# Graph attention over a random adjacency matrix: 2 MB adjacency loads, and a step whose parts stand in another order

## The chip, the cores and the metric

The kernel runs on one core of a Trainium2 chip. The number that counts is the device time of one execution in microseconds; where several runs were made, their median. The core's engines are TensorE (PE in the profile, its weight loads PEld), VectorE (DVE), ScalarE (ACT), GpSimd (POOL) and SyncE (SP), which only issues transfers here. Sixteen DMA engines move the data of all queues.

## The reference, cut to what matters

```python
h = relu(layernorm(x))                         # x: 8192 x 256, f32
support = (h @ weight)                         # 4 heads of 64 columns
f1 = support . weight_u; f2 = support . weight_v     # one number per node and head
scores = leaky_relu(f1[m] + f2[n], 0.2)        # for each pair n, m
masked = scores * adj                          # adj: 8192 x 8192, int32, ones with probability 0.000488
attn = softmax over m where masked != 0
out = attn @ support + bias + h @ proj_w.T + proj_b
return x + out
```

A row of the adjacency matrix has about four ones. The matrix itself has 8192 x 8192 x 4 bytes = 268 MB, and each byte of it is read once.

## The kernel before

The 8192 rows are worked in 64 tiles of 128 rows. All sizes of loads below are for 128 partitions.

**Reading the matrix.** SyncE issues `load_adj(t)` for each tile in order: four loads (`UNITS = 4`) of 1 MB, each with 8 KB for a partition, into six slots (`HELD = 6`). A slot can be loaded again when TensorE has read it. TensorE's `pack_places(t)` and `pack_unit(t, u)` turn the 8192 entries of a row into 1024 words by matmuls (16 for a tile, 4 for a unit), and the last matmul of a unit frees the slot (`s_adj_used`). VectorE's `pick_words(t)` finds the words that are not empty, and `split_words` makes columns of them.

**First stage** (up to about 230 us): sixteen times, four tiles of x are normalised, transposed and projected, the rows of `support` are stored in a table in HBM, and one tile of the matrix is packed beside it.

**Second stage**: 32 groups of two tiles (`GS = 2`), one group in each step `g` of the loop over `range(LATE)`, `LATE = 30`, and then two groups more, written out. In a step the engines work on four groups at a time:

- VectorE picks the one or two tiles that `picks[g]` names (2, 1, 2, 1, ..., and 2 in each of the last three), computes `one_hot(g)` and `list_spill(g)` for group g, `scores`, `row_maximum`, `shift` and `weigh` for g - 1, `output` for g - 2, and `list_own(g + 1)`, the indices of the first five neighbours of each row of group g + 1.
- TensorE computes `offsets(g)` and `edge_records(g)`, `row_scores(g - 1)`, `edge_refs(g - 1)`, `aggregate(g - 2, b)` (the weighted sum over a tile's gathered rows), and packs the tiles `t + 1` for `t` in `picks[g]`.
- GpSimd gathers rows of the table by indirect DMA: ten for a group by `gather_own` (five for each of the two tiles), after `list_own` and after ScalarE's `clear`, and two by `gather_spill`, after `list_spill`. Three groups of gathered rows (`RING = 3`) are held.
- ScalarE copies the edge records out of PSUM (`record_edges`), clears a ring slot, computes `distances(g + 1)` and the exponentials.

Each engine runs its part in the order in which it is written; semaphores tie the engines together. SyncE's stores of the output stand behind all loads of the matrix in its queue.

## Time and profile before

| | |
|---|---|
| median of 3 runs | 858.75 us (856.42 to 859.03) |
| the profiled execution | 857.76 us, of it a span of 855.9 us |
| TensorE busy | 712.2 us (83%) |
| VectorE busy | 644.8 us (75%) |
| GpSimd busy | 530.2 us (62%) |
| ScalarE busy | 129.5 us (15%) |
| moved by DMA | 329.82 MB, 385 GB/s over the span |
| of it SyncE's queue q1 | 286.28 MB, its packets 83.6% of the 16 engines' span |
| of it the gathers, q0 | 34.30 MB, 11.1% |

The profile gives an engine's busy time, the idle time in front of a group of instructions with what ended it, and for the DMA queues the packets, their bytes and the time that they took. A packet of the matrix is one partition's contiguous row of a load. The time of a packet runs until its data have moved, so a share of 1.00 says that each of the sixteen engines had a packet under way, and not at which rate.

### The profile page before, as it was taken

Reading aid. Unit: us, or ns where it says so; the run is one execution under the profiler, and the core shown is the slowest. Engines: PE = TensorE matmul, PEld = TensorE weight load, DVE = VectorE, ACT = ScalarE, POOL = GpSimd, SP = SyncE. Lnnn points to the kernel's source line nnn. Section 1 sums busy time; section 2 is a strip of 40 time slices with the busy share of each in tenths; the row PEclk is TensorE's granted clock in tenths of the full one; section 3 lists DMA queues with packets and bytes.
Section 4 is the critical chain, followed back from the end, with each engine's and each line's share of the span. In section 5 each row is a group of like instructions: output and inputs, shape, how many; then the busy total and the mean of one; then the engine's idle time right before and its main releaser. Section 6 shows DMA issues by size and latency. Waiting matters only on the chain.

```text
span 855.9 us, 11167 instructions
## 1 busy us (share of the span) xinstructions
PE 712.2 (83%) x3011; PEld 438.6 (51%) x3011; DVE 644.8 (75%) x2747; ACT 129.5 (15%) x468; POOL 530.2 (62%) x598
## 2 busy tenths in 40 slices
PE   2989999999957889777888888788888878888777
PEld 0656666666514454454545444455545445454455
DVE  4556666657446989879778797978879797889886
ACT  0223333333210001000001011000011100000010
POOL 4444455454467776776767667676776766676760
PEclk9999999999966879998888898887989899799888
DMA  8999999999999999999999999999999999999971
GB/s 317 419 417 396 415 409 420 416 420 406 425 408 393 385 397 394 401 405 393 399 387 376 389 370 398 384 406 388 397 396 381 403 382 407 378 384 388 404 308 51
DMA packets 63855, 329.82 MB, mean 385 GB/s; under 512 B 12795, under 2 KB 15560, under 8 KB 31024
## 3 DMA queue, kind: packets, MB, share of 16 engines
q1 hardware_dynamic: 43056, 286.28, 83.6%
q0 software_dynamic: 18432, 34.30, 11.1%
q10 hardware_dynamic: 2304, 8.52, 2.4%
q8 instruction: 25, 0.41, 0.2%
q14 instruction: 38, 0.31, 0.1%
HBM read 328.99 MB, written 16.91 MB: 404 GB/s over the span
## 4 chain that ended last, share of the span: by engine, by line
PE 44%; DVE 26%; DMA 23%; issue 3%; POOL 2%; ACT 1%; POOLq 0%; ACTq 0%; SPq 0%
DMA adj_raw<-in_adj 20%; PE ps_words L400 12%; PE ps_agg L461 9%; PE ps_agg L381 7%; PE ps_two L381 6%; DVE att L937 6%; PE ps_two L400 5%; DVE cand L791 3%; DVE base L947 3%; DMA att<-support_table,idx 2%; PE ps_score L445 2%; DMA att<-in_x 1%; PE ps_words L392 1%; DMA support_table<-att 1%; PE ps_list L371 1%
## 5 line engine op out<-in xcount | busy, mean ns | idle before, releaser
L719 POOL DMA_INDIRECT att<-support_table,idx x384 | 418.4, 1090 | 184.5 <-issue 105.0
L400 PE MATMUL ps_words<-adj_raw,pack_w 128*128 128x512 fp8e4 x640 | 187.0, 430 | 25.9 <-DMA adj_raw<-in_adj 25.9
L461 PE MATMUL ps_agg<-att,ident 128*128 128x260 f32 x640 | 183.0, 441 | 6.7 <-DVE att L937 6.7
L461 PEld LDWEIGHTS ps_agg<-att,ident 128*128 128x128 f32 x640 | 139.7, 225 | 41.6 <-issue 17.3
L400 PE MATMUL ps_two<-adj_raw,pack_w 128*128 128x512 fp8e4 x384 | 112.6, 442 | 22.2 <-DMA adj_raw<-in_adj 22.2
L400 PEld LDWEIGHTS ps_words<-adj_raw,pack_w 128*128 128x128 bf16 x640 | 62.3, 106 | 124.7 <-DMA adj_raw<-in_adj 38.9
L791 DVE MAX8 cand<-ps_words 128x8 f32<-128x128 f32 x320 | 67.2, 281 | 66.3 <-PE ps_words L400 66.3
L937 DVE TENSOR_TENSOR att<-att 128x1536 f32<-128x1536 f32 x64 | 109.6, 1751 | 1.2 <-ACT att L623 1.2
L710 POOL COPY record<-att 128x8 f32<-128x8 f32 x64 | 13.5, 212 | 116.9 <-ACT att L567 116.9
L400 PEld LDWEIGHTS ps_two<-adj_raw,pack_w 128*128 128x128 bf16 x384 | 38.5, 111 | 83.9 <-DMA adj_raw<-in_adj 31.8
L381 PE MATMUL ps_agg<-w_all,hT 128*128 128x260 f32 x256 | 63.0, 389 | 4.0 <-ACT hT L563 3.8
L381 PE MATMUL ps_two<-w_all,hT 128*128 128x260 f32 x256 | 62.0, 385 | 2.6 <-ACT hT L563 2.6
L947 DVE SCALAR_TENSOR_TENSOR base<-ps_agg,rdenom,base 128x64 f32<-128x64 f32 x256 | 55.0, 277 | 2.3
L381 PEld LDWEIGHTS ps_two<-w_all,hT 128*128 128x128 f32 x256 | 47.3, 190 | 11.3 <-ACT hT L563 3.1
L381 PEld LDWEIGHTS ps_agg<-w_all,hT 128*128 128x128 f32 x256 | 46.0, 190 | 13.4 <-ACT hT L563 7.8
L708 POOL TENSOR_TENSOR base<-att,bias_row 128x256 f32<-128x256 f32 x64 | 46.9, 733 | 0.1
L712 POOL TENSOR_TENSOR base<-base,att 128x256 f32<-128x256 f32 x64 | 46.6, 728 | 0.0
L791 DVE MAX8 cand<-ps_two 128x8 f32<-128x128 f32 x192 | 40.2, 280 | 6.2 <-PE ps_two L400 6.0
L617 ACT ACTIVATE edge_rec<-ps_list 128x34 f32<-128x34 f32 x32 | 6.4, 199 | 249.0 <-PE ps_list L438 249.0
L871 DVE TENSOR_SCALAR edge_slot<-edge_rec,edge_at 128x2 f32<-128x2 f32 x32 | 7.5, 234 | 47.2 <-ACT edge_rec L617 47.2
L445 PE MATMUL ps_score<-score_slot,onehotT 128*128 128x44 f32 x128 | 23.6, 322 | 19.6 <-DVE score_slot L903 19.6
L461 PE MATMUL ps_agg<-att,onehotT 128*128 128x260 f32 x128 | 39.0, 386 | 0.0
(118 smaller groups left out, 796.8 us busy)
## 6 DMA issues: line engine op xcount, KB each, us to landing
adj_raw<-in_adj SPq DMA_DIRECT2D x256, 1024.0 KB, 13.5
support_table<-att ACTq DMA_DIRECT2D x16, 520.0 KB, 8.7
att<-in_x SPq DMA_DIRECT2D x16, 512.0 KB, 6.4
out<-base SPq DMA_DIRECT2D x15, 512.0 KB, 15.1
att<-support_table,idx POOLq DMA_INDIRECT x384, 6.3
out<-base SPq DMA_DIRECT2D x4, 128.0 KB, 1.9
w_all<-in_proj_wT SPq DMA_DIRECT2D x2, 128.0 KB, 5.6
w_all<-in_weight SPq DMA_DIRECT2D x2, 128.0 KB, 5.8
```

Of the source, the lines that this page charges most:

```text
L371: mm = nc.tensor.transpose(ps_t[t % 2][:, c * P:(c + 1) * P], xhat[:, t // LOAD % 2, t % LOAD, c * P:(c + 1) * P], ident[:])
L381: mm = nc.tensor.matmul(ps_proj[t % 2][:, half, 0:ROW], hT[:, t % 2, c * P:(c + 1) * P], w_all[:, c, half, :], start=(c == 0), stop=(c == ...
L400: mm = nc.tensor.matmul(ps_words[buffer_of(t)][:, k * 512:(k + 1) * 512], pack_w[:, u * UT + s, :], adj_low[:, n % HELD, s, k * 512:(k + 1 ...
L445: mm = nc.tensor.matmul(ps_row[:, b].rearrange("p k h -> p (k h)"), onehotT[:, g % RING, b], score_slot[:, b].rearrange("p k h -> p (k h)" ...
L461: mm = nc.tensor.matmul(ps_agg[:, b, 0:ROW], ident[:] if k < OWN else onehotT[:, g % RING, b], gathered[:, g % RING, b, k], start=(k == 0) ...
L708: pool.tensor_tensor(base[:, t], x_in[:, g % 2, q, :], bias_row[:], ALU.add).then_inc(s_basev, 1)
L710: pool.tensor_copy(record[:, t, R_F2:].rearrange("p (a h) -> p a h", a=2), stage[:, g % 2, :, q, HF:])
L712: pool.tensor_tensor(base[:, t], base[:, t], stage[:, g % 2, 0, q, 0:HF], ALU.add).then_inc(s_based, 1)
L719: pool.indirect_dma_start(gathered[:, g % RING, b, k, :], None, table, bass.IndirectOffsetOnAxis(idx[:, g % RING, b, k:k + 1], 0), bounds_ ...
L791: last = v.max(cand[:, s * 8:(s + 1) * 8], ps[:, s * SEG:(s + 1) * SEG])
L937: v.tensor_tensor(r, r, rows[:, :, HF:].unsqueeze(3).to_broadcast([P, BLOCKS, H, HD]), ALU.mult).then_inc(s_weighted, 1)
L947: last = v.scalar_tensor_tensor(base[:, t, cols], ps_agg[:, b, cols], rdenom[:, b, h:h + 1], base[:, t, cols], ALU.mult, ALU.add)
```

## The change

- `UNITS = 2`, `HELD = 4`: a tile is loaded in two loads of 2 MB, each with 16 KB for a partition, and four slots hold 8 MB (before, six held 6 MB). A unit has 8 matmuls now. To make room, `spare`, `uv_row`, `projb_row` and `place_hi` lie in the last tiles of `base` and `hT` in `onehot`, which are not used at the same time.
- The order of a step for groups before `SOLO` (27): TensorE does `edge_records(g)`, both aggregations, `row_scores`, `edge_refs`, `offsets(g + 1)`, and packs last, now the tiles `t + 2`; tile 17 is packed before the loop. VectorE does `one_hot(g)` first, then picks, `list_spill(g)`, `scores(g - 1)`, and `list_own(g + 1)` in the middle of the step. ScalarE clears and does `distances(g + 1)` ahead of the exponentials.
- From group 27 on the two tiles of a group are listed, cleared and gathered singly; before, only the last two groups were.

```diff
-UNITS = 4
-HELD = 6
+UNITS = 2
+HELD = 4
...
+    AHEAD = [g for g in range(G) if FIRST + sum(counts[:max(g - 1, 0)]) >= groups[g][0] + GS]
+    SOLO = len(AHEAD)
+    assert AHEAD == list(range(SOLO)) and RING <= SOLO < LATE
+
+    def listed(g, b):
+
+        return g + 1 if g < SOLO else SOLO + GS * (g - SOLO) + b + 1
...
-        spare = sb("spare", [P, 4, HF])
...
-        uv_tmp = spare[:].rearrange("p (q c) d -> p q c d", q=2)
+
+        uv_tmp = base[:, TILES - 4:].rearrange("p (q c) d -> p q c d", q=2)
+        uv_row = base[:, TILES - 6:TILES - 4]
+        projb_row = base[:, TILES - 7]
+        place_hi = base[0:2, TILES - 9:TILES - 7].rearrange("p a d -> p (a d)").bitcast(BF16)
...
+        hT = onehot[:].rearrange("p a b m -> p a (b m)")
...
-                    if q > 0:
-                        pack_unit(g + 1, q - 1)
+                    if q > 0 and q % (LOAD // UNITS) == 0:
+                        pack_unit(g + 1, q // (LOAD // UNITS) - 1)
...
             pe.wait_ge(s_staged, TILES)
+            pack_places(FIRST + 1)
+            for u in range(UNITS):
+                pack_unit(FIRST + 1, u)
+            offsets(0)
             for g in range(LATE):
-                new = [t + 1 for t in picks[g]]
-                offsets(g)
-                pack_places(new[0])
-                for u in range(UNITS // 2):
-                    pack_unit(new[0], u)
-                if g >= 2:
-                    aggregate(g - 2, 0)
-                edge_records(g)
+                if g >= SOLO:
+                    offsets(g)
+                else:
+                    edge_records(g)
+                for b in range(GS):
+                    if g >= 2:
+                        aggregate(g - 2, b)
+                if g >= SOLO:
+                    edge_records(g)
                 if g > 0:
                     row_scores(g - 1)
-                for u in range(UNITS // 2, UNITS):
-                    pack_unit(new[0], u)
-                if g > 0:
                     edge_refs(g - 1)
-                if g >= 2:
-                    aggregate(g - 2, 1)
-                for t in new[1:]:
-                    pack_places(t)
-                    for u in range(UNITS):
-                        pack_unit(t, u)
+                if g + 1 < SOLO:
+                    offsets(g + 1)
+                for t in picks[g]:
+                    if t + 2 < TILES - 1:
+                        pack_places(t + 2)
+                        for u in range(UNITS):
+                            pack_unit(t + 2, u)
...
-                if g + 1 == LATE:
-                    clear(LATE, 0, 1)
+                if g + 1 >= SOLO:
+                    for b in range(GS):
+                        clear(g + 1, b, 1)
+                elif g + 1 >= RING:
+                    clear(g + 1)
+                if g + 1 < SOLO:
+                    distances(g + 1)
                 if g > 0:
                     exponential(g - 1)
-                if g + 1 == LATE:
-                    clear(LATE, 1, 1)
-                elif g + 1 >= RING:
-                    clear(g + 1)
-                distances(g + 1)
+                if g + 1 >= SOLO:
+                    distances(g + 1)
...
-            def gather_own(g, n, at=0, size=GS):
-                pool.wait_ge(s_idx_own, n)
-                pool.wait_ge(s_cleared, n)
-                for b in range(at, at + size):
+            def gather_own(g, *only):
+                for b in only or range(groups[g][1]):
+                    pool.wait_ge(s_idx_own, listed(g, b))
+                    pool.wait_ge(s_cleared, listed(g, b))
                     for k in range(OWN):
                         gather(g, b, k)
...
-            for g in range(LATE - 1):
-                gather_own(g, g + 1)
-                gather_spill(g)
...
+            for g in range(SOLO):
+                gather_own(g)
+                if g + 1 < SOLO:
+                    gather_spill(g)
+            for g in range(SOLO, G):
+                gather_own(g, 0)
+                gather_spill(g - 1)
+                gather_own(g, 1)
+            gather_spill(G - 1)
...
             list_own(0)
             for g in range(LATE):
+
+                due = [t for t in picks[g] if g + 1 >= SOLO and t < groups[g + 2][0]]
+                if 0 < g < SOLO:
+                    one_hot(g)
+                if g + 1 >= SOLO and groups[g + 1][0] < picks[g][0]:
+                    list_own(g + 1, 0, 1)
                 n = pick_words(picks[g][0], 0)
-                if g + 1 == LATE:
-                    picked = split_words(picks[g][0], 1, n)
-                    list_own(LATE, 0, 1)
+                if due:
+                    picked = split_words(due[0], 1, n)
+                    list_own(g + 1, due[0] % GS, 1)
                 if g == 0:
 
                     dve.wait_ge(s_based, TILES)
-                one_hot(g)
+                if g == 0 or g >= SOLO:
+                    one_hot(g)
+                else:
+                    list_spill(g)
                 if g > 0:
                     scores(g - 1)
-                list_spill(g)
+                if g == 0 or g >= SOLO:
+                    list_spill(g)
+                if g + 1 < SOLO:
+                    list_own(g + 1)
+                if g >= 2:
+                    output(g - 2, 0)
                 if g > 0:
                     row_maximum(g - 1)
-                if g >= 2:
-                    output(g - 2, 0)
...
-                    list_own(g + 1)
```

What the order of instructions shows, for a step in the middle of the second stage. TensorE before, one step with two new tiles (`ps_list<-spilled` is `offsets`, `ps_words<-adj_raw` a pack, `ps_agg` an aggregation, `ps_list<-record` is `edge_records`, `ps_score` first `row_scores` and then `edge_refs`):

```order
L429 MATMUL ps_list<-spilled,before 128x2
L430 MATMUL ps_list<-spilled,minus_mid 128x2
L392 MATMUL ps_words<-place,ones_row 128x512 x2
L400 MATMUL ps_words<-adj_raw,pack_w 128x512 x8
L461 MATMUL ps_agg<-att,ident 128x260 x5
L461 MATMUL ps_agg<-att,onehotT 128x260
L438 MATMUL ps_list<-record,onehot 128x17 x2
L445 MATMUL ps_score<-score_slot,onehotT 128x44 x2
L400 MATMUL ps_words<-adj_raw,pack_w 128x512 x8
L452 MATMUL ps_score<-row_ref,onehot 128x4 x2
L461 MATMUL ps_agg<-att,ident 128x260 x5
L461 MATMUL ps_agg<-att,onehotT 128x260
```

TensorE after, the same kind of step, up to the first of its packs (there follow the places and the 16 matmuls of a second tile):

```order
L448 MATMUL ps_list<-record,onehot 128x17 x2
L471 MATMUL ps_agg<-att,ident 128x260 x5
L471 MATMUL ps_agg<-att,onehotT 128x260
L471 MATMUL ps_agg<-att,ident 128x260 x5
L471 MATMUL ps_agg<-att,onehotT 128x260
L455 MATMUL ps_score<-score_slot,onehotT 128x44 x2
L462 MATMUL ps_score<-row_ref,onehot 128x4 x2
L439 MATMUL ps_list<-spilled,before 128x2
L440 MATMUL ps_list<-spilled,minus_mid 128x2
L402 MATMUL ps_two<-place,ones_row 128x512 x2
L410 MATMUL ps_two<-adj_raw,pack_w 128x512 x16
```

The pack of 8 and 8 matmuls that stood among the small products is one piece of 16 at the step's end, behind both aggregations, `row_scores`, `edge_refs` and the next step's `offsets`.

VectorE before, where a step's own neighbours are listed (`held`, `idx`, `spilled` are `list_own`; `record<-codes_rest` ends `split_words`):

```order
L817 MAX record<-codes_rest 128x8
L815 MAX record<-codes 128x8
L816 MATCH_REPLACE codes_rest<-record,codes 128x128
L817 MAX record<-codes_rest 128x8
L847 TENSOR_SCALAR held<-record 128x22
L851 TENSOR_SCALAR idx<-record 128x2x5
L855 TENSOR_REDUCE spilled<-held 128x2
L943 TENSOR_SCALAR denom<-ps_agg 128x4
```

VectorE after, at the same function (`score_slot` ends `scores`):

```order
L917 TENSOR_TENSOR score_slot<-slot_hot,score 128x88
L861 TENSOR_SCALAR held<-record 128x22
L865 TENSOR_SCALAR idx<-record 128x2x5
L869 TENSOR_REDUCE spilled<-held 128x2
L957 TENSOR_SCALAR denom<-ps_agg 128x4
L958 RECIPROCAL rdenom<-denom 128x4
```

`list_own(g + 1)` moved from behind the splitting of the step's words to behind `scores(g - 1)`, with one output of group g - 2 behind it and the splitting later.

## Rows read from the trace of the kernel before

**Rows 1.** The page: span, and its slices of 21.4 us
```profile
span 855.9 us, 11167 instructions
...
PEclk9999999999966879998888898887989899799888
DMA  8999999999999999999999999999999999999971
GB/s 317 419 417 396 415 409 420 416 420 406 425 408 393 385 397 394 401 405 393 399 387 376 389 370 398 384 406 388 397 396 381 403 382 407 378 384 388 404 308 51
```

**Rows 2.** Windows: stretch, length, busy us, TensorE clock, DMA share, GB/s
```profile
60.00:210.00 150.00, 146.94 (x688) 99.51 (x687) 95.87 (x401) 47.92 (x107) 75.60 (x143) 1.00 1.01 412
260.00:790.00 530.00, 439.54 (x1817) 261.80 (x1818) 442.99 (x1898) 54.14 (x280) 371.53 (x341) 0.87 1.00 391
484.00:490.00 6.00, 5.74 (x25) 3.79 (x24) 2.05 (x11) 0.20 (x1) 3.88 (x5) 0.81 1.02 402
505.00:510.00 5.00, 5.00 (x21) 3.53 (x19) 4.36 (x23) 0.58 (x3) 3.78 (x5) 0.82 1.01 346
530.00:535.00 5.00, 4.27 (x20) 2.04 (x19) 4.83 (x15) 1.40 (x7) 2.59 (x2) 1.00 1.02 402
```

**Rows 3.** DMA queues between 24.6 and 34 us
```profile
q1 hardware_dynamic: 540, 3.92, 100.6%
```

**Rows 4.** DMA queues between 92 and 97 us
```profile
DMA packets 403, 2.10 MB, mean 421 GB/s; under 512 B 35, under 2 KB 35, under 8 KB 259
...
q1 hardware_dynamic: 282, 1.61, 78.3%
```

**Rows 5.** DMA queues between 260 and 790 us
```profile
q1 hardware_dynamic: 24226, 176.43, 84.1%
q0 software_dynamic: 16329, 30.44, 15.9%
```

**Rows 6.** Line 863, the one-hot of a step: ns min/median/max, first and last start
```profile
L863 DVE TENSOR_SCALAR onehot<-distance,reach x64: 268/278/305, 232.3 to 824.7; 128x128 f32<-128x128 f32 x64
```

**Rows 7.** The chain of waits between 480 and 535 us, the longest pieces
```profile
467.39 13.26 DMA adj_raw<-in_adj
480.69 1.89 PE ps_two L400 x4
...
494.91 3.33 DVE att L937 x2
...
506.21 12.10 DMA adj_raw<-in_adj
518.36 1.89 PE ps_words L400 x4
```

**Rows 8.** Waits between 240 and 800 us: total, times, longest
```profile
DVE edge_slot L871 <- ACT edge_rec L617: 44.6, 13, 5.2
...
PE ps_list L438 <- DVE onehot L863: 23.7, 15, 1.6
...
DVE score L889 <- DMA att<-support_table,idx: 13.9, 3, 10.8
...
DVE cand L791 <- PE ps_words L400: 7.5, 7, 3.5
DVE cand L791 <- PE ps_two L400: 5.4, 7, 1.3
```

**Rows 9.** Groups between 260 and 790 us, the gathers
```profile
L719 POOL DMA_INDIRECT att<-support_table,idx x341 | 372.0, 1091 | 158.8 <-issue 93.4 <-DVE idx L851 44.4 <-ACT att L590 17.4
```

**Rows 10.** The page: DMA issues, KB each, us to landing
```profile
support_table<-att ACTq DMA_DIRECT2D x16, 520.0 KB, 8.7
...
att<-support_table,idx POOLq DMA_INDIRECT x384, 6.3
```

**Rows 11.** SyncE's DMA issues between 780 and 856 us
```profile
797.33 38.28 SPq L340 DMA_DIRECT2D out<-base  x15
```

**Rows 12.** Timeline of TensorE between 790 and 856 us
```profile
814.40 3.37 PE L400 MATMUL ps_two<-adj_raw,pack_w 128*128 128x512 fp8e4 x8
```

More of the change, by code:

```diff
@@ L115, in gat_kernel @@
         w_all = sb("w_all", [P, KC, 2, ROW])
-        uv_row = sb("uv_row", [P, 2, HF])
         bias_row = sb("bias_row", [P, HF])
-        projb_row = sb("projb_row", [P, HF])
         eps_col = sb("eps_col", [P, 1])
@@ L122, in gat_kernel @@
         place = sb("place", [2, WORDS], BF16)
-        place_hi = sb("place_hi", [2, WORDS], BF16)
         bit_mask = sb("bit_mask", [P, BITS], I32)
@@ L131, in gat_kernel @@
         row_no = sb("row_no", [P, P])
-        hT = sb("hT", [P, 2, KC * P])
         stats = sb("stats", [P, LOAD, 6])
@@ L276, in gat_kernel @@
             att[:, P + q * H * P:P + (q + 1) * H * P].rearrange("p (h m) -> p h m", h=H) for q in range(5))
-        dn_out, dn_x, dn_xhat, dn_base = (spare[:, q, :] for q in range(4))
+        dn_out, dn_x, dn_xhat, dn_base = (base[:, q, :] for q in range(4))
         dn_rest = att[:, P + 5 * H * P:]
@@ L323, in _ @@
                              (bias_row[:, :], bias),
-                             (projb_row[:, :], proj_b.rearrange("(o d) -> o d", o=1))):
+                             (projb_row, proj_b.rearrange("(o d) -> o d", o=1))):
                 sp.dma_start(dst, src.to_broadcast([P, HF])).then_inc(s_w_in, 16)
@@ L699, in _ @@
             pool.wait_ge(s_w_in, 16 * W_LOADS)
-            const(pool.tensor_tensor(bias_row[:], bias_row[:], projb_row[:], ALU.add))
+            const(pool.tensor_tensor(bias_row[:], bias_row[:], projb_row, ALU.add))
             assert const.n == POOL_CONSTS
@@ L952, in _ @@
             for g in range(LATE):
+                due = [t for t in picks[g] if g + 1 >= SOLO and t < groups[g + 2][0]]
[3 more added lines that the diff above has]
+                    list_own(g + 1, 0, 1)
                 n = pick_words(picks[g][0], 0)
-                if g + 1 == LATE:
-                    picked = split_words(picks[g][0], 1, n)
-                    list_own(LATE, 0, 1)
+                if due:
+                    picked = split_words(due[0], 1, n)
+                    list_own(g + 1, due[0] % GS, 1)
                 if g == 0:
                     dve.wait_ge(s_based, TILES)
-                one_hot(g)
+                if g == 0 or g >= SOLO:
+                    one_hot(g)
+                else:
+                    list_spill(g)
                 if g > 0:
                     scores(g - 1)
-                list_spill(g)
+                if g == 0 or g >= SOLO:
[4 more added lines that the diff above has]
+                    output(g - 2, 0)
                 if g > 0:
                     row_maximum(g - 1)
-                if g >= 2:
-                    output(g - 2, 0)
                 for t in picks[g][1:]:
-                    n = pick_words(t, 0 if g + 1 == LATE else 1)
+                    n = pick_words(t, 0 if due else 1)
                 if g > 0:
                     shift(g - 1)
-                if g + 1 == LATE:
-                    picked = split_words(picks[g][1], 1, n)
-                    list_own(LATE, 1, 1)
+                if due:
+                    for t in picks[g][1:]:
+                        picked = split_words(t, 1, n)
+                        if t in due:
+                            list_own(g + 1, t % GS, 1)
                 else:
                     picked = split_words(picks[g][0], len(picks[g]), n)
-                    list_own(g + 1)
                 if g >= 2:
```

8 lines of the change are left out of this document (removed).

## The prediction

> **What bounds the kernel now.** I read the page's slices first: the DMA share stands at 9 tenths or more from the second slice to the last but two, while the rate falls from about 415 GB/s in the first stage to about 390 in the second [rows 1]. By windows: 412 GB/s at a share of 1.01 in the first stage, with TensorE busy for 146.9 of 150 us; 391 GB/s at 1.00 between 260 and 790 us, with TensorE busy 439.5 and VectorE 443.0 of 530 us [rows 2]. So the first stage has two bounds at once, DMA and TensorE, and in the second the DMA engines always have a packet under way but move 5% less.
>
> Why less? A packet that waits for its data counts as busy. In 505:510 the share is 1.01 and the rate 346 GB/s; in 484:490 and 530:535 the share is 1.02 and the rate 402 [rows 2]. The first is what a matrix queue that has run dry and starts again looks like. The chain of waits tells who let it run dry: a load is under way 13.26 us, lands at 480.65, TensorE reads it, and through both engines, with `weigh` (3.33 us) in the middle, the chain comes back to a slot that is free only at 506.21, 25.5 us later; the next load takes 12.10 us [rows 7]. One turn of the loop is 37.7 us and covers three tiles, two steps. The one-hots say the same: 31 steps from 232.3 to 824.7 us, 19.1 us a step, 38.2 a pair [rows 6]. VectorE waits in this stage 44.6 us for edge records, 13.9 for gathers and 12.9 for packed words, 71 of 560 us; TensorE waits 23.7 us for one-hots [rows 8]. Without its waits VectorE would need 38.2 x 489/560 = 33.3 us for a pair. So the second stage is a loop of waits (38.2) lying a little above the DMA work, and both engines have some reserve below it.
>
> How much is DMA work? Where neither queue is dry, 402 GB/s; the 207.3 MB of 260:790 (391 GB/s x 530 us) would take 515.7 us at that rate, 14.3 us less, 16 us over the whole stage of 592 us. That is 37.2 us for a pair.
>
> **The change part by part.**
>
> *2 MB loads.* The bytes stay; a partition's row is 16 KB, so the matrix has 16,384 packets instead of 32,768. The price of a packet's beginning is seen by comparing sizes. Alone, 3.92 MB take 100.6% of 9.4 us in 16 engines: 479 packets of 8 KB, 316 ns each, their small companions included [rows 3]. Between 92 and 97 us the queue also has x rows of 4 KB: 403 - 259 = 144 packets of 8 KB, and (1.61 - 1.18) MB / 4096 = 105 of 4 KB in 62.6 us of engine time, so (62.6 - 45.5)/105 = 163 ns each [rows 4]. Twice 163 less 316 is 10 ns a packet; 16,384 x 10 ns / 16 = 10 us. The counts are rough (packets cut by the window), so the bounds are 0 and 10 us, and a quarter of it lies in the first stage, where TensorE bounds too. I take 6.
>
> *8 MB in slots instead of 6, and the new order.* They act on the same thing, the loop. In the new order `weigh`, the pick and the splitting no longer stand between a landed load and the next free slot: TensorE reads the load, does `edge_records`, VectorE `list_spill`, `scores`, `list_own`, one output, `row_maximum`, then TensorE packs and frees. Of the 25.5 us of the old chain I estimate that 12 to 16 are left (weigh 3.3, a pick and a splitting go, one aggregation too). While they pass, 6 to 8 MB are under way, 15 us or more at 391 GB/s. By the order shown above, the one-hot first in a step takes away TensorE's 23.7 us, and the pick behind it covers the copy of the edge records that VectorE waited 44.6 us for. Bounds: nothing (a new loop of the same length) and 16 us (never dry). Since VectorE's 33.3 is well below 37.2 I take 11, and a pair of 37.1 us with the packets' part.
>
> *Listing in the middle, late tiles singly.* The gathers start some 9 us earlier in a step. GpSimd issues one in (372.0 + 93.4)/341 = 1.36 us, 12 in a step, 16.4 of 19.1 us [rows 9]; they land after 6.3 us [rows 10]. It hides 13.9 us of waits that are counted above. For the last groups it costs VectorE a second splitting in three steps, under 1 us each, beside the loads. Cover gone, 2 us.
>
> *`clear` and `distances` ahead of the exponentials.* ScalarE is busy 129.5 us in all; the exponential has VectorE's splitting and an output (some 3 us) as cover. If `edge_refs` is late, what waits behind `distances` is `weigh`. Nothing to 3 us; I take nothing.
>
> *Start and end.* SyncE's stores follow all loads: they are issued from 797.33 on [rows 11], TensorE's last pack starts at 814.40 and takes 3.37 us [rows 12], and the 38 us behind it are the chain of the last two groups, written as before. The last unit must land as 2 MB before its 8 matmuls start, and so must the first ones: some 1 us together.
>
> **The sum.** 857.8 (the profiled execution) - 6 - 11 + 1 = 841.8. The median of the three runs lies 1 us above that execution, so 843.
>
> **The rivals.**
>
> *Slower: the gathers starve behind 16 KB packets.* If an engine takes its queues in turn, packet by packet, a gather's packet waits for one packet of the matrix each time. A gather has 16,329/341/16 = 3 packets in each engine, of 83 ns on average (0.159 x 530 x 16 / 16,329), and the matrix's take about 330 [rows 5]: 3 x 413 = 1.24 us, just below the 1.36 at which GpSimd issues. With 16 KB it is 3 x (632 + 83) = 2.15 us, 25.7 us for 12, in a step of 18.6. For it: the table's store, 520 KB, which alone would take 1.3 us at 415 GB/s, lands after 8.7 us [rows 10], so queues do share by turns. Against: the matrix has only 1.5 x 2 x 9 = 27 packets a step in each engine against 36 of the gathers, so its queue is dry before the gathers are through, and what is left goes fast (9 x 83 ns if already issued); and `list_own` stands earlier. It decides from the point where VectorE waits for gathers more than its reserve of 1.9 us a step. At worst the 9 left over come at GpSimd's pace, 4.1 us a step with little else moving: 17.4 + 4.1 = 21.5 us, +74 us. I take a third of it, +24 us: 882, since the queue that is dry lets the other drain. The Trainium skill ("DMA: Bandwidth & Descriptors", section "Queues, rings and completion order") states just such turns at packet granularity; what a packet of 16 KB does to the turns no run here shows yet.
>
> *Slower too: packs last.* In a step TensorE frees no slot for both aggregations and the small products. It is busy 439.5 us for 27.7 steps, 15.9 us a step [rows 2]; a step's 24 pack matmuls are 10 us of it where eight take 3.37 us [rows 12] and about half that at the full clock, so 6 to 11 us are left without a free slot. With 15 us under way that is covered; if gathers are late as well it is not. It goes with the case above.
>
> *No change: the loop finds another way to the same length*, TensorE's part being the longer one when its clock is low. 853 to 860.
>
> *Faster still:* packets worth 10, never dry, and TensorE's first stage relieved: 857.8 - 10 - 16 - 3 = 829.
>
> **Chances.** The forecast (835 to 853) 0.47; faster still (824 to 835) 0.17; no change and little gain (853 to 862) 0.13; slower (862 to 930) 0.23. Range for 8 in 10: 826 to 880. Within 0.3% of 858.75 is what a measurement here can't tell from no change (856.2 to 861.3): faster 0.67, same 0.10, slower 0.23.
>
> **What the profile will show.** Half as many large packets in q1, none under 8 KB but stores and x. A rate of 400 GB/s or more between 260 and 790 us, and a pair of steps of 37.1 us (one-hots 18.5 apart). VectorE's wait for edge records mostly gone, TensorE waiting for the matrix instead of for one-hots. If the gathers' landing goes from 6.3 to 10 us or more and VectorE waits for them, the slower rival is at work; if their landing stays below 8, the turns are not by packet. I am wrong in the sum if the first stage changes by over 3 us, or the tail behind the last pack by over 3.

## The result and the profile after

The changed kernel takes 868.43 us (median of 6 runs, 866.37 to 870.83) beside 857.8 for the kernel before (6 runs): a ratio of 1.0131, 95% interval 1.0113 to 1.015. It is 10.6 us slower where 16 us less were forecast. The profiled execution has a span of 865.1 us, 9.2 more than before [rows 1].

The page of the changed kernel: span, TensorE's granted clock in tenths, DMA share in tenths and GB/s of 40 slices of 21.6 us, the matrix's queue, and the loads (KB each, median us from issue to landing).

```profile
span 865.1 us, 11092 instructions
...
PEclk9999999999976998798989968997998989987888
DMA  8999999999999999899989999998999999997961
GB/s 319 426 424 416 405 410 423 413 410 419 433 416 373 381 412 405 351 366 407 415 344 412 411 374 361 410 412 338 413 412 380 362 407 414 388 414 272 396 256 50
...
q1 hardware_dynamic: 24624, 286.27, 80.6%
...
adj_raw<-in_adj SPq DMA_DIRECT2D x128, 2048.0 KB, 15.5
```

Before, the DMA row was 9 from the second slice to the last but two, and no slice between the first and the last two lay under 370 GB/s [rows 1]. Now 8 of the 26 slices from the 13th to the 38th have 338 to 374 GB/s, and one has 272. The windows (length; busy us of PE, PEld, DVE, ACT and POOL; granted clock, DMA share, GB/s) and the DMA queues of 260:790 say the same in sums:

```profile
60.00:210.00 150.00, 146.92 (x684) 99.09 (x685) 91.94 (x401) 47.62 (x106) 75.02 (x143) 1.00 1.00 413
260.00:790.00 530.00, 416.35 (x1771) 251.07 (x1772) 434.93 (x1872) 52.28 (x278) 369.35 (x339) 0.87 0.96 385
```

```profile
DMA packets 28467, 204.04 MB, mean 385 GB/s; under 512 B 8294, under 2 KB 9404, under 8 KB 17877
...
q1 hardware_dynamic: 11878, 172.86, 79.5%
q0 software_dynamic: 16549, 30.74, 16.6%
```

The first stage is as it was, 413 against 412 GB/s [rows 2]. In 260:790 the DMA engines are idle for 4% of the time, where they were never idle before, and 204.04 MB are moved in place of 207.3 (391 GB/s for 530 us). The missing 3.3 MB are 8.4 us at that rate, but that is not the difference of the spans: q1 had moved more before 260 us (96.90 MB against 95.54), and the matrix is complete no later than before, as the next fences show. TensorE and VectorE, too, are less busy than before (416 and 435 us against 440 and 443) in this window.

The last load of the matrix, from its issue to its landing, before and then after:

```profile
L317 SPq DMA_DIRECT2D adj_raw<-in_adj x1: 327/327/327, 797.0 to 797.0; - x1
...
DMA to landing us min/median/max: 17.9/17.9/17.9
```

```profile
L327 SPq DMA_DIRECT2D adj_raw<-in_adj x1: 328/328/328, 794.8 to 794.8; - x1
...
DMA to landing us min/median/max: 19.2/19.2/19.2
```

It lands at 814.9 us before and at 814.0 after, 0.9 us earlier. From there to the end of the span it was 41.0 us and is now 51.1. So the matrix comes in as fast as before, and the whole loss stands behind its last load. Before, TensorE's last pack ran from 814.40 to 817.8 us, as the load came in [rows 12]; now it ends at 826.9, 12.9 us behind the landing:

```profile
823.72 3.17 PE L410 MATMUL ps_two<-adj_raw,pack_w 128*128 128x512 fp8e4 x8
```

Behind that pack's end there are 38.2 us, and 38.1 before. The repeat e5 has the same picture: landing at 815.0, end at 866.8.

What do the engines wait for? Waits between 240 and 800 us (total, times, longest), and two pieces of the chain of waits between 480 and 540 us:

```profile
DVE score L903 <- DMA att<-support_table,idx: 53.3, 10, 8.8
PE ps_score L455 <- DVE score_slot L917: 50.9, 9, 12.0
...
PE ps_list L448 <- DVE onehot L877: 27.5, 18, 2.9
...
DVE edge_slot L885 <- ACT edge_rec L631: 10.6, 2, 10.3
```

```profile
489.79 21.79 DMA att<-support_table,idx
...
511.61 0.20 DVE score L903
```

VectorE waits 53.3 us for gathers (13.9 before), and TensorE waits 50.9 us for `score_slot`, which VectorE can make only then. The wait for edge records fell, from 44.6 to 10.6 us, that for one-hots (23.7) did not [rows 8]. In sum VectorE waits no less: 81.9 us for all that it waited for between 240 and 800 us, 76.4 before. Where the chain before showed loads of 13.26 and 12.10 us [rows 7], it now shows one gather of 21.79 us from issue to landing. The one-hots, 31 steps from the first to the last start:

```profile
L877 DVE TENSOR_SCALAR onehot<-distance,reach x64: 270/280/285, 234.5 to 833.9; 128x128 f32<-128x128 f32 x64
```

That is 19.34 us a step, against 19.1 before [rows 6] and 18.5 in the forecast.

### The profile page after: what moved, and what is told of

It is laid out like the page before. It is cut to its first block, busy times and chain, and to the rows that moved or that the text cites. A ratio compares the mean times of both kernels' runs of the same rounds, so it can differ in the third digit from the quotient of the medians.

```text
span 865.1 us, 11092 instructions
## 1 busy us (share of the span) xinstructions
PE 697.9 (81%) x3011; PEld 432.8 (50%) x3011; DVE 642.5 (74%) x2764; ACT 127.0 (15%) x471; POOL 532.0 (61%) x598
## 4 chain that ended last, share of the span: by engine, by line
PE 37%; DVE 24%; DMA 20%; issue 9%; POOL 8%; ACT 1%; SPq 1%; POOLq 0%; ACTq 0%
DMA att<-support_table,idx 15%; PE ps_words L410 8%; PE ps_agg L471 8%; POOL att L735 8%; PE ps_agg L391 6%; PE ps_two L391 6%; DVE att L951 5%; PE ps_two L410 3%; DVE cand L805 3%; DVE base L961 2%; DMA att<-in_x 2%; DMA adj_raw<-in_adj 2%; PE ps_words L402 1%; DMA support_table<-att 1%; PE ps_score L462 1%
## 5 line engine op out<-in xcount | busy, mean ns | idle before, releaser
L410 PE MATMUL ps_words<-adj_raw,pack_w 128*128 128x512 fp8e4 x640 | 174.0, 425 | 0.7 <-DMA adj_raw<-in_adj 0.7
L471 PE MATMUL ps_agg<-att,ident 128*128 128x260 f32 x640 | 166.1, 410 | 3.7 <-DVE att L951 3.7
L471 PEld LDWEIGHTS ps_agg<-att,ident 128*128 128x128 f32 x640 | 127.9, 204 | 24.0 <-issue 3.8
L391 PE MATMUL ps_agg<-w_all,onehot 128*128 128x260 f32 x256 | 63.0, 389 | 4.1 <-ACT onehot L577 4.1
L391 PE MATMUL ps_two<-w_all,onehot 128*128 128x260 f32 x256 | 61.6, 384 | 1.0 <-ACT onehot L577 1.0
L462 PE MATMUL ps_score<-row_ref,onehot 128*128 128x4 f32 x128 | 23.6, 290 | 41.2 <-DVE row_ref L932 41.2
L391 PEld LDWEIGHTS ps_agg<-w_all,onehot 128*128 128x128 f32 x256 | 46.1, 190 | 13.4 <-ACT onehot L577 7.9
L391 PEld LDWEIGHTS ps_two<-w_all,onehot 128*128 128x128 f32 x256 | 47.3, 191 | 8.2 <-ACT onehot L577 1.8
L455 PEld LDWEIGHTS ps_score<-score_slot,onehotT 128*128 128x128 f32 x128 | 21.0, 218 | 55.9 <-DVE score_slot L917 54.7
L903 DVE TENSOR_TENSOR score<-att,record 128x40 f32<-128x40 f32 x32 | 6.3, 197 | 53.3 <-DMA att<-support_table,idx 53.3
L448 PE MATMUL ps_list<-record,onehot 128*128 128x17 f32 x128 | 20.0, 271 | 30.9 <-DVE onehot L877 30.8
```

The lines of the kernel that those rows point to most:

```text
L391: mm = nc.tensor.matmul(ps_proj[t % 2][:, half, 0:ROW], hT[:, t % 2, c * P:(c + 1) * P], w_all[:, c, half, :], start=(c == 0), stop=(c == ...
L410: mm = nc.tensor.matmul(ps_words[buffer_of(t)][:, k * 512:(k + 1) * 512], pack_w[:, u * UT + s, :], adj_low[:, n % HELD, s, k * 512:(k + 1 ...
L448: mm = nc.tensor.matmul(ps_rec[:, b], onehot[:, g % 2, b], record[:, first + b, OWN:R_F1], start=True, stop=True)
L455: mm = nc.tensor.matmul(ps_row[:, b].rearrange("p k h -> p (k h)"), onehotT[:, g % RING, b], score_slot[:, b].rearrange("p k h -> p (k h)" ...
L462: mm = nc.tensor.matmul(ps_ref[:, b], onehot[:, g % 2, b], row_ref[:, b], start=True, stop=True)
L471: mm = nc.tensor.matmul(ps_agg[:, b, 0:ROW], ident[:] if k < OWN else onehotT[:, g % RING, b], gathered[:, g % RING, b, k], start=(k == 0) ...
```

## The experiments

All times are medians, each beside the kernel before on the same chip. Six chips came up. On three (e5 to e11, e18) the kernel before takes 856.5 to 856.7 us, close to the 857.8 beside the changed kernel's own result; on three others (e1 to e4, e12 to e17) 869.7 to 873.6. On the latter the engines of every variant start late for reasons that the profile does not name (last section), so ratios are compared within the first kind. "Order: changed" in the table means all of it, the late part from step 26 on included.

| run | order | loads, slots | this, us | before, us | ratio (95%) |
|---|---|---|---|---|---|
| e5 | changed | 2 MB, 4 | 868.74 | 856.45 | 1.015 (1.0133 to 1.0167) |
| e6 | changed | 1 MB, 8 | 865.99 | 856.45 | 1.0113 (1.0094 to 1.0132) |
| e7 | changed | 1 MB, 6 | 872.7 | 856.45 | 1.0188 (1.0164 to 1.0211) |
| e18 | before | 2 MB, 4 | 927.29 | 856.65 | 1.0815 (1.0785 to 1.0845) |
| e4 | before | 1 MB, 8 | 870.2 | 871.81 | 0.9987 (0.9956 to 1.0017) |
| e8 | changed, late part as before | 1 MB, 8 | 860.1 | 856.57 | 1.0042 (1.0024 to 1.0061) |
| e9 | as e8, late lists single | 1 MB, 8 | 867.73 | 856.57 | 1.0138 (1.0111 to 1.0165) |
| e10 | as e8, late packs last | 1 MB, 8 | 862.41 | 856.57 | 1.0077 (1.0049 to 1.0104) |
| e11 | before, late part changed | 1 MB, 6 | 870.36 | 856.57 | 1.0156 (1.0125 to 1.0188) |

### The parts of the change apart: e1 to e7, e18

The changed order with smaller loads (e1 and e6: `HELD = 8`; e7: `HELD = 6`; e5 is the changed kernel itself):

```diff
-UNITS = 2
-HELD = 4
+UNITS = 4
+HELD = 8
```

The order of before with the changed kernel's memory layout (e3, e14 and e18: 2 and 4; e4: 4 and 8):

```diff
-UNITS = 4
-HELD = 6
+UNITS = 2
+HELD = 4
...
-                    if q > 0:
-                        pack_unit(g + 1, q - 1)
+                    if q > 0 and q % (LOAD // UNITS) == 0:
+                        pack_unit(g + 1, q // (LOAD // UNITS) - 1)
```

And the changed kernel with each 2 MB slot filled by two transfers whose rows are 8 KB (e2 and e15):

```diff
+                    E = UT * WORDS // PARTS
+                    for h in range(PARTS):
+                        sp.dma_start(adj_raw[:, n % HELD].rearrange("p s e -> p (s e)")[:, h * E:(h + 1) * E],
+                                     adj_v[t // LOAD, t % LOAD, u][:, h * E:(h + 1) * E]).then_inc(
+                                         s_adj_in[n % HELD], 16)
```

Expected of e1:

> The changed kernel with UNITS = 4, HELD = 8: the new order and 8 MB of slots, but loads of 1 MB with rows of 8 KB. Theory (turns by packet: a gather's three packets in an engine each wait for one packet of the matrix): gathers land in 6 to 8 us again, VectorE's wait for gathers falls from 53 us to under 10, and the order's gain shows: 840 to 850 us. Rival (the new order itself is what costs, since all packs stand at the end of a step): 860 us or more, with gathers landing fast.

of e2:

> The changed kernel with its slots of 2 MB and its order, but each slot filled by two transfers of 1 MB with rows of 8 KB. It differs from the changed kernel in the size of a packet alone. Theory (turns by packet): like the run with 1 MB loads, 840 to 852 us, gathers landing in 6 to 8 us. Rival (a slot of 2 MB comes free too late, whatever its packets): as the changed kernel, 865 to 872 us.

of e3:

> The order of before with UNITS = 2, HELD = 4 (the memory laid out as in the changed kernel). Theory (turns by packet): the old order has less slack for gathers than the new one (it lists a group's own neighbours at the end of a step), so it suffers more from 16 KB packets: 875 us or more, VectorE waiting over 60 us for gathers. Rival (the new order is the cost): 855 us or less.

of e4:

> The order of before with UNITS = 4, HELD = 8: two more slots of 1 MB are all that is new. If more memory for loads removes dry spells of the matrix queue by itself: 845 to 852 us. If the loop of waits sets the pace whatever is loaded ahead: 855 to 858 us, as before.

These four ran beside 871.81 us for the kernel before. e4 gave 870.2: two slots more change nothing in the old order, on a chip of the second kind. e3 gave 934.87, a ratio of 1.071 (1.0641 to 1.0778). e1 (924.5, runs from 900 to 944) and e2 (942, 914 to 948) scattered too widely to be read, on a chip of the second kind. e5 to e7 ran on one of the first.

> The changed kernel as it is, timed beside the kernel of before on this chip. The kernel of before took 871.8 us on the chip of the first four runs and 857.8 on the one of the result, so the control is needed before runs of different chips are compared. If the loss belongs to the change: a ratio of 1.01 to 1.02. If it depends on the chip (the first four runs showed engines starting 3 to 5 us after the last thing that they waited for): another ratio, and with it more such late starts.

> The new order with UNITS = 4, HELD = 8 once more, now beside the changed kernel itself on one chip. It differs from it in the size of loads, slots and packets alone. Theory (turns by packet cost the gathers): faster than the changed kernel by 1% or more, gathers landing within 8 us. Rival (the order's loop is the cost, as 924 us in the first run of it suggests): slower than the changed kernel, by up to 5%.

> The new order with the loads and slots of before (UNITS = 4, HELD = 6): the order alone. With all packs at the end of a step, 6 MB last 15 us. If that is too little: 1 to 3% slower than the new order with 8 slots of 1 MB. If what costs is not dry slots: the same as with 8 slots.

e5 repeats the result. The order alone, late part included (e7), costs 16.3 us; with two slots more (e6) 9.5; with the same 8 MB in loads of 2 MB (e5) 12.3. With six slots the last load lands late, at 823.3 us in e7. In e6 and e7 hardly any gather is waited for; the window 260:790 and the two waits of VectorE, e6 first:

```profile
260.00:790.00 530.00, 429.73 (x1781) 260.57 (x1780) 440.15 (x1880) 51.87 (x279) 371.88 (x339) 0.86 0.99 389
```

```profile
DVE edge_slot L885 <- ACT edge_rec L631: 34.6, 12, 11.8
...
DVE row_score L926 <- PE ps_score L455: 23.9, 15, 1.9
...
DVE score L903 <- DMA att<-support_table,idx: 1.8, 1, 1.8
```

```profile
260.00:790.00 530.00, 425.85 (x1767) 254.24 (x1768) 436.14 (x1870) 51.77 (x278) 369.52 (x338) 0.86 0.98 383
```

```profile
DVE edge_slot L885 <- ACT edge_rec L631: 36.9, 13, 11.2
...
DVE score L903 <- DMA att<-support_table,idx: 5.3, 2, 2.9
```

VectorE waits 1.8 and 5.3 us for gathers with 8 KB rows, 53.3 with 16 KB rows. The waits of VectorE only changed their place, though: in e6 they are 78.0 us in sum (before 76.4), with 23.9 us for `ps_score` that it did not have before. And e6 is not faster than the kernel before either: its share is 0.99 and its rate 389 GB/s, as before (1.00 and 391 [rows 2]). Its chain between 260 and 790 us, by line, is that of a kernel that waits for the matrix; the changed kernel's (the second fence) is that of one that waits for gathers and for their issue:

```profile
by line: DMA adj_raw<-in_adj 45.1%; PE ps_agg L471 15.4%; PE ps_words L410 8.8%; PE ps_two L410 5.7%; DVE att L951 3.2%; issue 2.6%; PE ps_score L462 1.8%; PE ps_list L448 1.7%; DVE cand L805 1.5%; DVE base L961 1.2%; DVE row_max L929 1.2%;
```

```profile
by line: DMA att<-support_table,idx 24.3%; issue 12.7%; POOL att L735 11.2%; PE ps_agg L471 8.4%; DVE att L951 6.9%; PE ps_two L410 4.3%; DVE cand L805 4.2%; PE ps_words L410 3.7%; DVE base L961 3.0%; PE ps_score L462 1.5%; DVE codes_rest L
```

For the loads alone e14 repeated e3, and e15 repeated e2; both fell on the same chip as e1 to e4 (beside 871.84 us).

> As e3 (the order of the kernel before, loads of 2 MB in 4 slots), on a chip that doesn't disturb it as the first one did. If 16 KB rows delay the gathers and whole-tile halves free the slots late, it is slower by itself: 1.01 to 1.03 (865 to 882). If the 7% of e3 came of that chip alone and loads of 2 MB cost nothing: 0.995 to 1.004.

> As e2 (the changed kernel, each 2 MB slot filled by two transfers of 1 MB with rows of 8 KB). If the 16 KB rows cost something by the late landing of the gathers, the wait of VectorE for gathers (53.3 us in the changed kernel) falls below 30 and the ratio from 1.013 to 1.005 to 1.010. If the saving of the fewer packets (3.033 against 2.98 us per MB says no saving) is about as large: 1.010 to 1.016, as e6 with its 1.0113.

e14: 933.04, ratio 1.0715 (1.069 to 1.0739). e15: 922.33 (909 to 937), no ratio; but in its profile, as in that of e2, VectorE never waits for a gather. e14 could still have been the chip's doing:

> The kernel of e3 and e14: the order of before, loads of 2 MB in 4 slots. With the new order 2 MB cost 2 to 3 us over 1 MB (e5 868.7, e6 866.0, same chip). If that is their price in the old order too: 1.002 to 1.006. If the old order, which frees half a tile at a time and then waits for records and aggregations, leaves a slot of 2 MB empty for longer: 1.01 to 1.03, VectorE's wait for gathers above 40 us and the DMA share between 260 and 790 us below 0.97. Where the kernel before takes 869 or more, 1.07 again says only that this chip is of the other kind.

On a chip of the first kind the old order with loads of 2 MB in four slots takes 927.29 us, 70.6 more than before. I had put e3 down to the chip, and that was wrong: it is the kernel, whose profile here has no such late starts. The slices of e18, its window, its waits, and two pieces of its chain:

```profile
DMA  8999999999989989799797979797898979897971
GB/s 330 426 367 415 404 413 411 415 412 430 427 317 358 413 304 401 292 359 361 299 394 308 406 277 417 302 400 288 355 361 310 409 289 402 303 416 282 400 284 47
```

```profile
260.00:790.00 530.00, 374.45 (x1604) 226.05 (x1604) 391.61 (x1667) 47.43 (x249) 337.09 (x303) 0.84 0.89 348
```

```profile
PE ps_score L444 <- DVE score_slot L902: 124.8, 25, 20.3
DVE score L888 <- DMA att<-support_table,idx: 108.7, 13, 20.4
```

```profile
442.08 13.62 DMA att<-support_table,idx
...
484.38 14.05 DMA att<-support_table,idx
```

In the later half every second or third slice falls to some 280 to 310 GB/s. VectorE waits for gathers 13 times, up to 20.4 us, 108.7 us in all; the pieces of 13.62 and 14.05 us are gathers under way. A gather between 260 and 790 us lands after 2.5, 8.1 and 14.0 us (shortest, median, longest), and before after 3.9, 6.3 and 8.0. TensorE, which waits for `score_slot` meanwhile, frees no slot, and the matrix's load breaks off: a DMA share of 0.99 from 450 to 456 us, 0.30 from 456 to 460. The loads of 2 MB are thus the dangerous part of this change, and with the new order they cost far less: 12.3 us instead of 70.6. That this is because it lists earlier is an argument; no run moves the list alone. Nor does a run on the old order part the rows of 16 KB from the slots of 2 MB, which come free half a tile at a time.

### The late part: e8 to e11

The one-hots of steps 26 and 27 start at 729.5 and 754.6 us in the changed kernel, 25.1 us apart, against 19.4 before. There (from `SOLO = 27` on) lists and clears become single and TensorE's order differs from that of before in another way. e8 gives e6 the late part of before on all engines; e9 that of TensorE alone, e10 that of lists and clears alone; e11 gives the kernel before the changed late part. The edits, TensorE's first (in e8 and e9), then that of the lists (e8 and e10), cut to their core:

```diff
+            for g in range(SOLO, LATE):
+                new = [t + 1 for t in picks[g]]
+                offsets(g)
+                pack_places(new[0])
+                for u in range(UNITS // 2):
+                    pack_unit(new[0], u)
+                aggregate(g - 2, 0)
+                edge_records(g)
+                row_scores(g - 1)
+                for u in range(UNITS // 2, UNITS):
+                    pack_unit(new[0], u)
+                edge_refs(g - 1)
+                aggregate(g - 2, 1)
```

```diff
-                due = [t for t in picks[g] if g + 1 >= SOLO and t < groups[g + 2][0]]
+                due = picks[g] if g + 1 == LATE else []
...
-                if g + 1 >= SOLO and groups[g + 1][0] < picks[g][0]:
-                    list_own(g + 1, 0, 1)
...
                     picked = split_words(picks[g][0], len(picks[g]), n)
+                    if g + 1 >= SOLO:
+                        list_own(g + 1)
```

> The changed order up to step 26 with loads of 1 MB in 8 slots (as e6), and from there on everything as the kernel before does it: TensorE packs the step's first tile in halves ahead of each of the two aggregations, and lists and clears go by pairs (singly only for the last two steps). e6 was 1.0113 of the kernel before and lost most of it between the one-hots of steps 25 and 30 and behind them: the last matrix load landed as early as before, yet the end came 8 to 10 us later behind it. Theory A (the loss is the late part: TensorE packs two tiles in one piece ahead of the aggregations and the records, so everything that hangs on a step stands behind 10 us of packs): ratio 1.001 to 1.004 (857 to 860), the one-hots of steps 26 and 30 apart by 82 us as before. Theory B (the loss is in the early steps, the order before step 26): still 1.008 to 1.013. Theory C (single lists and clears: GpSimd waits for the clears, gathers come later): the same as A here, told apart by e9 and e10.

> As e8, but only TensorE's order of the late part is that of before; lists and clears stay single from step 26 on. A: 1.001 to 1.004 (857 to 860), like e8. C: 1.009 to 1.013 (864 to 867), like e6. B: 1.008 to 1.013.

> As e8, but only the lists and clears of the late part are by pairs as before; TensorE keeps the changed order (both aggregations first, packs last). A: 1.009 to 1.013, like e6. C: 1.001 to 1.004, and GpSimd's wait for the clears (13.3 us in e6 between 725 and 825 us) gone. If the pair lists were what the packs-last order needs least, since they come at the step's end, it could also be slower than e6: up to 1.02.

> The kernel before (1 MB, 6 slots) with the late part of the changed kernel alone, on all engines, from step 26 (lists) and 27 (TensorE) on. A or C: most of the loss comes with it, 1.006 to 1.012 (862 to 867). B: 1.000 to 1.003 (856 to 859).

Theory A does not carry the loss: with TensorE's late order of before and single lists e9 is at 1.0138. With pair lists that order is worth 2.3 us (e10 to e8), within the intervals of the two. Theory C holds for the greater part: pair lists take 7.6 us off with the old TensorE order (e9 to e8, same chip) and 3.1 with the new one (0.0036 of 856.5, e6 to e10, two chips). What remains in e8, 0.4% or 3.6 us, is the early steps' (B) share by subtraction, with the seam between the two orders in it; the one-hot of step 25 comes at 710.2 to 712.8 us in e6 to e10, and at 707.3 before. e11 loses more than the whole change, 13.8 us; but at its seam TensorE packs one tile more than a step normally does, so a part of it is the seam's.

What single lists cost can be seen in part in the window from the one-hot of step 26 to that of 27, here of before, after, e9, e8 and e10:

```profile
726.60:746.00 19.40, 14.94 (x61) 7.54 (x62) 17.61 (x77) 1.92 (x10) 13.10 (x12) 0.82 0.98 374
```

```profile
729.50:754.60 25.10, 20.99 (x92) 12.89 (x93) 23.65 (x111) 2.08 (x11) 18.47 (x17) 0.93 0.99 393
```

```profile
731.40:756.80 25.40, 19.66 (x78) 13.12 (x78) 23.78 (x112) 2.08 (x11) 18.50 (x17) 0.84 0.90 344
```

```profile
731.40:755.70 24.30, 19.90 (x78) 13.10 (x78) 20.04 (x90) 1.83 (x10) 12.05 (x11) 0.86 0.82 324
```

```profile
731.90:753.10 21.20, 19.16 (x91) 12.44 (x92) 20.04 (x91) 1.88 (x10) 12.09 (x11) 1.00 0.93 366
```

VectorE is busy 23.65 of 25.1 us in the changed kernel and 23.78 of 25.4 in e9, with 111 and 112 instructions; with pair lists 20.04 us with 90 or 91. So splitting and listing tile by tile gives VectorE 3.7 us more in a step that it nearly fills. How much of that is time is not settled: with TensorE's new order the window shrinks from 25.4 us (e6) to 21.2 (e10), with its old one only from 25.4 (e9) to 24.3 (e8), where VectorE is no longer full. Before, VectorE has 17.61 us of work here: for the other 2.4 us the likely reason is the one-hot's place, first in the step up to 26 and behind the pick from 27 on, so that a pick more lies between the two.

A second cost can be GpSimd's. With single lists `clear` stands ahead of `exponential`, and may wait for aggregations. Waits between 725 and 825 us of e8, of e9 and of the changed kernel (L616 and L604 are `clear`):

```profile
ACT att L616 <- PE ps_agg L471: 6.9, 3, 4.2
...
POOL att L750 <- ACT att L616: 2.1, 2, 1.8
```

```profile
ACT att L616 <- PE ps_agg L471: 32.2, 6, 8.1
...
POOL att L747 <- ACT att L616: 10.8, 5, 3.8
```

```profile
POOL att L735 <- ACT att L604: 10.6, 2, 5.6
...
ACT att L604 <- PE ps_agg L471: 7.9, 3, 2.9
```

GpSimd waits 10.6 to 13.3 us for a clear with single lists (the changed kernel, e9, e6) and 2.1 and 4.7 with pairs (e8, e10). ScalarE's 32.2 us belong to e9 alone, where TensorE's old order meets single lists; in the changed kernel they are 7.9. What these waits are worth is not shown: the profiled executions of e8 and e9 both took 864.27 us, e8's near its slowest and e9's its fastest, so the 7.6 us between the medians are not in these two traces.

### What did not settle: e12, e13, e16, e17

These move TensorE's late `offsets` ahead of most of the packs (e12, again as e16 and e17), and the first half of each step's first pack between the aggregations and the row scores (e13, with loads of 1 MB). The edit of e12:

```diff
-                if g >= SOLO:
-                    offsets(g)
-                else:
+                if g < SOLO:
                     edge_records(g)
...
                             pack_unit(t + 2, u)
+                            if g + 1 >= SOLO and t == picks[g][0] and u + 1 == UNITS // 2:
+                                offsets(g + 1)
```

> The changed kernel (2 MB) with one thing moved: from step 26 on, TensorE's offsets of the next pair stand behind the first half of the step's first pack, no longer behind all packs of the step. In the changed kernel ScalarE's mid waited 7.5 us for them in step 26 and 5.1 in step 27, and the one-hots of 26 and 27 are 25.1 us apart against 19.4 before. Theory D (offsets behind the packs are what the late part costs): the distance of 26 and 27 falls to 19 to 21 us, ratio from 1.013 to 1.003 to 1.008 (859 to 863). Rival (the records and scores of the older pair bound the step anyway): 1.011 to 1.015, and the time only moves from ScalarE's wait for offsets to VectorE's wait for gathers or TensorE's for VectorE.

> Loads of 1 MB in 8 slots, the changed order with the offsets as in e12, and in every step the first half of the first pack between the aggregations and the row scores, where TensorE waited 50.9 us for VectorE's score_slot in the changed kernel. If the early 0.4% comes of packs bunched at the end of the step, the one-hot of step 25 comes at 705 to 708 us (e6 712.8, before 707.3) and the ratio is 0.993 to 1.002. If not, it is that of e12 with 1 MB loads, 1.002 to 1.008; if the half pack (2 to 4 us) delays the row scores in each step, 1.01 or more.

> e12 again, on another chip if it falls so (on the one with 872 us for the kernel before: again 1.05 to 1.08, and nothing is learned). Theory D: the one-hots of steps 26 and 27 are 19 to 21 us apart instead of 25, ratio 1.003 to 1.008 (859 to 863). Rival: 1.011 to 1.015, the wait only moves.

> The kernel of e12 and e16. Where the kernel before takes 855 to 858: theory D 1.003 to 1.008 with the one-hots of steps 26 and 27 apart by 19 to 21 us; the rival 1.011 to 1.015, the wait only moved. Where it takes 869 or more: 1.04 to 1.08 again, and nothing is learned of D.

e12 gave 934.08 (beside 871.84), e16 916.38 (869.74), e17 943.88 (873.6), e13 963.42 (871.84). All four fell on chips of the second kind, so theory D is neither shown nor refuted; the windows above, with VectorE busy for 94% of step 26, speak against it, but not strongly: in e8 it is busy for 82% of a step of 24.3 us. Whether packs in halves would give the early 3.6 us back is open too.

## Why the prediction was wrong

**What bounds the kernel: the step that failed.** I took the second stage for a loop of waits that could be shortened by 11 of 16 us, since the rate there was 391 and not 402 GB/s and VectorE waited 71 us. Two things were wrong in that.

First, up to the last load the kernel goes at about the pace of the DMA engines, and not at that of the waits. The last load was to land some 17 us earlier; it lands 0.9 us earlier (814.0 against 814.9). In e6, with 8 MB of slots and gathers on time, share and rate stayed at 0.99 and 389, and VectorE's waits added up to 78.0 us instead of 76.4: they moved to other places and did not shrink. The 402 GB/s of a 6 us window was not a rate that the mix of matrix and gathers kept up in any run here. The term of -11 was worth nothing: with 8 slots and the late part as before, the new order costs 3.6 us (e8), and with its own late part 9.5 (e6).

Second, I took the stretch behind the last load as given, but for 1 us. The 38 us behind TensorE's last pack held. But that the last pack follows the last load closely did not: TensorE's last pack now ends 12.9 us behind the landing, where it ended 2.9 behind it. That is the whole loss of the profiled execution, and e6 to e11 put the greater part of it into the late steps.

**Fewer packets, -6.** With the new order the capacity is there, and does not become time. Queues and bytes of e6 in 260:790:

```profile
DMA packets 40462, 206.35 MB, mean 389 GB/s; under 512 B 9507, under 2 KB 10604, under 8 KB 19009
...
q1 hardware_dynamic: 24097, 175.42, 82.9%
q0 software_dynamic: 16324, 30.48, 16.0%
```

98.9% of 530 us for 206.35 MB are 2.540 us of DMA time a MB; in the changed kernel 79.5% and 16.6%, together 96.1%, for 204.04 MB are 2.496. The difference is 0.044 us a MB, some 10 us over the second stage's 231 MB (391 GB/s for 592 us): the upper bound that I gave. But 3.9% of the window, 20.7 us, went idle. With the old order the saving is not seen: e18, with rows of 16 KB too, needs 88.4% of 530 us for 184.69 MB, 2.537 a MB. Loads of 2 MB cost 2.7 us on balance (e5 beside e6).

**The slower rival.** I gave "the gathers starve behind 16 KB packets" 0.23 and put it at 882. The starving came, 53.3 us of waits; but it is not what makes this kernel 10.6 us slower, since e6 has hardly any of it and loses 9.5. That the time fell into this rival's band, 862 to 930, is in part luck. What I held against it, that the matrix's queue runs dry early and that `list_own` stands earlier, may be what keeps its price at 2.7 us with the new order. With the old order 2 MB loads cost +70.6 us, close to the worst case of +74 that I had worked out for the new one and then divided by three. The Trainium skill ("DMA: Bandwidth & Descriptors", "Queues, rings and completion order") states that a DMA engine takes turns between its queues packet by packet. The waits agree with it: 1.8 us in e6 and 56.4 in e5, in the same order and with the same 8 MB in slots, while rows, loads and slots are twice as large. e2 and e15 have 2 MB slots and 8 KB rows and show no such wait, where e12, e16 and e17 with rows of 16 KB show 20.6, 10.3 and 11.2 us. That speaks for the row rather than the slot, though on chips of the second kind and with `offsets` moved in the latter three. In the Trainium skill's section such a packet typically holds some 9 to 17 descriptors; whether it is what the profile counts as a packet, one row, is not shown. My sign for turns by packet, gathers landing after 10 us or more, was not met: the median is 8.1 in e18, and the profile gives none for the changed kernel.

**Late tiles singly, under 1 us each.** This was mis-sized: 3.1 to 7.6 us in all (e6 to e10, e9 to e8), against 2 us of waits and under 1 us a step. I costed a second splitting as work beside the loads; in step 26 VectorE is busy for 23.65 of 25.1 us. `clear` ahead of the exponential was costed at nothing to 3 and taken as nothing; what it costs by itself was not tried.

**Start and end, +1.** The first stage held (413 against 412 GB/s), and the tail behind the last pack (38.2 against 38.1 us). The first one-hot comes 2.2 us later (234.5 against 232.3), which I had not costed; that TensorE now packs tile 17 ahead of `offsets(0)` would explain it, and wasn't tried by itself.

Of the signs, half the large packets and VectorE waiting for gathers came; 400 GB/s and 18.5 us a step did not. The chance of 0.67 for faster rested on the loop of waits alone.

## What to carry to other kernels

Before counting a wait as a gain, look at what is busy meanwhile. Here the DMA share was 1.00 beside VectorE's 76 us of waits; another order moved the waits and left the last load's landing where it was. Where a stream bounds the kernel, also look at how far the engines are behind it when it ends: that distance, 41 us before and 51 after, is paid in full.

When a large stream shares the DMA engines with small transfers that somebody waits for, try larger loads together with the order that they meet: here 2 MB loads cost 8% with one order and 0.3% more than 1 MB loads with another. An order that splits work into smaller pieces to start things early pays for it in the engine that is fullest in that very step, whatever its average says.

## What the runs showed of the hardware

The chips are of two kinds for these programs: 856.5 us for the kernel before on three, 869.7 to 873.6 on three. On the latter the variants lose far more: e6's kernel, 865.99 us on the first kind, took 924.5 on a chip of the second (e1). There engines start late with nothing in the profile that they wait for. In e1, ScalarE's waits for "issue" and "remote" (sources that the trace can't name) before `edge_rec`, which e6 does not have at all:

```profile
ACT edge_rec L631 <- issue: 62.4, 9, 8.8
...
ACT edge_rec L631 <- remote: 57.1, 5, 13.2
```

The longest such wait is in e13, in the middle of its chain, while the DMA share was 0.96:

```profile
262.66 24.42 another core or an unknown queue
...
287.10 0.17 ACT mid L622
```

What delays these engines, and why on these chips only, stays open.
